# A latent-attention block with 16 tiles: two spreads as VectorE block transposes instead of TensorE products, and the scaling by one over the sums on VectorE behind the addition

## The reference, cut to what matters

```python
x = x + xattn(layernorm(x), ctx)       # 16 heads of 32; keys = values = context rows; softmax over 257
x = x + self_attn(layernorm(x), ...)   # low-rank q and kv, rope, 16 heads of 32, softmax over 32
x = x + ffn(layernorm(x), ...)         # 8 experts, each row takes the one with the largest gate

# xattn, per batch and head:
sim  = q @ k.T * 32 ** -0.5            # 32 x 257
out  = softmax(sim) @ k                # 32 x 32
```

## Time and profile before

| | |
|---|---|
| time, median of 3 runs | 858.45 us (856.07 to 860.0) |
| the profiled execution: span from its first to its last instruction | 854.9 us |
| what lies around that span, against the median | 3.5 us |
| mean granted clock of TensorE over the span | 0.984 of full speed |
| the chain that ended last, by engine | PE 61%, DVE 16%, POOL 7%, issue 6%, ACT 4%, DMA 3% |
| transfers from and to HBM | 151 GB/s over the span |

### The profile page before, as it was taken

The page is one execution under the profiler, slowest core; times in us unless marked ns, Lnnn a source line. Parts: engine busy times, 40 slices in busy tenths (PEclk is TensorE's granted clock), DMA queues, the critical chain, the costliest instruction groups (busy, mean ns, idle before and its releaser), DMA issues.

```text
span 854.9 us, 26663 instructions
## 1 busy us (share of the span) xinstructions
PE 768.7 (90%) x10666; PEld 577.6 (68%) x10666; DVE 610.8 (71%) x1211; ACT 422.9 (49%) x1062; POOL 313.9 (37%) x638
## 2 busy tenths in 40 slices
PE   4897979989899898988989899898988789999998
PEld 3544767768676786867768676786876556666664
DVE  3477677777877768787777877778645557788883
ACT  2353464554645556464554645546322354555552
POOL 2013533333234242333233234243220435876642
PEclk9999999999999999999999999999999899999999
DMA  9955654656646565484554636564061499454430
GB/s 277 331 130 100 132 153 118 143 140 130 153 112 160 124 162 138 100 184 120 148 142 117 163 110 152 128 159 101 3 222 51 140 375 388 163 172 140 144 115 3
DMA packets 113850, 129.16 MB, mean 151 GB/s; under 512 B 13951, under 2 KB 80767, under 8 KB 113729
## 3 DMA queue, kind: packets, MB, share of 16 engines
q1 hardware_dynamic: 105984, 109.35, 47.7%
q0 software_dynamic: 5520, 16.26, 5.6%
q10 hardware_dynamic: 2224, 1.86, 0.8%
HBM read 114.85 MB, written 14.42 MB: 151 GB/s over the span
## 4 chain that ended last, share of the span: by engine, by line
PE 61%; DVE 16%; POOL 7%; issue 6%; ACT 4%; DMA 3%; SPq 3%; DVEq 0%; POOLq 0%
PE bank L500 10%; PE bank L1560 8%; PE bank L502 8%; PE bank L501 8%; PE bank L494 4%; PE scores L541 3%; PE scores L551 3%; PE bank L565 2%; PE scores L1538 2%; PE scores L1540 2%; PE scores L1539 2%; DVE negmax L1031 2%; PE bank L605 2%; POOL soft L1315 2%; POOL operand_lo L1292 2%
## 5 line engine op out<-in xcount | busy, mean ns | idle before, releaser
L826 ACT ACTIVATE prob<-scores,negmax 128x257 f32<-128x257 f32 x256 | 118.2, 477 | 42.0 <-DVE negmax L1031 41.3
L500 PE MATMUL bank<-qkv_hi,operand_hi 128*128 128x396 f32 x256 | 99.3, 388 | 4.3 <-DVE operand_lo L1035 4.2
L1031 DVE TENSOR_REDUCE negmax<-scores 128x2 f32<-128x514 f32 x128 | 82.1, 683 | 22.2 <-PE scores L541 22.2
L1021 DVE STREAM_TRANSPOSE k_t<-keys 128x512 f32<-128x512 f32 x128 | 88.3, 691 | 5.6 <-DMA keys<-in_ctx 5.5
L501 PE MATMUL bank<-qkv_lo,operand_hi 128*128 128x396 f32 x256 | 88.1, 344 | 0.0
L502 PE MATMUL bank<-qkv_hi,operand_lo 128*128 128x396 f32 x256 | 87.8, 343 | 0.0
L1560 PE MATMUL bank<-w_all,hidden 128*128 x184 | 82.8, 592 | 0.6 <-ACT hidden L1613 0.6
L551 PE MATMUL scores<-consts,prob 128*128 128x128 f32 x512 | 77.6, 276 | 1.6 <-ACT prob L826 1.6
L565 PEld LDWEIGHTS bank<-prob_t,context 128*32 128x32 f32 x4096 | 47.0, 113 | 42.9 <-issue 34.9
L1656 DVE TENSOR_TENSOR w_lo<-w_all,w_hi 128x512 fp32r<-128x512 f32 x89 | 73.3, 882 | 0.2
L551 PEld LDWEIGHTS scores<-consts,prob 128*128 128x128 f32 x512 | 63.2, 144 | 9.6 <-ACT prob L826 2.5
(11 more groups left out here) (249 smaller groups left out, 1705.5 us busy)
## 6 DMA issues: line engine op xcount, KB each, us to landing
keys<-in_ctx SPq DMA_DIRECT2D x256, 128.0 KB, 4.4
context<-in_ctx SPq DMA_DIRECT2D x64, 512.0 KB, 4.6
w_all<-in_L_ffn_W SPq DMA_DIRECT2D x16, 1024.0 KB, 12.3
b<-in_L_ffn_b SPq DMA_DIRECT2D x23, 256.0 KB, 3.6
norm_scratch<-norm SPq DMA_DIRECT2D x16, 256.0 KB, 2.0
x_tile<-in_x SPq DMA_DIRECT2D x8, 256.0 KB, 4.9
x_pair<-in_x SPq DMA_DIRECT2D x8, 256.0 KB, 4.7
x_scratch<-x_tile SPq DMA_DIRECT2D x8, 256.0 KB, 2.5
```

Source lines behind the costliest of these rows:

```text
L500: pe.matmul(to, op_hi[op][:, c, :], w_hi[name][:, c, columns], start=(c == 0), stop=False)
L826: act.activation(prob[pair][:, gg, :], scores[:, g, 0:J], ACT.Exp, bias=negmax[b % 2][:, g:g + 1], accum_out=sums[t % 2][:, g, bl:bl + 1]) ...
L1021: dve.transpose(dst, src).then_inc(keys_turned, 1)
L1031: dve.tensor_reduce(negmax[b % 2][:, 2 * pair:2 * pair + 2], scores[:, 2 * pair:2 * pair + 2, 0:J], AX.X, ALU.max, negate=True).then_inc(m ...
```

## The change

The spreads leave TensorE. VectorE's block transpose, which turns each block of 32 x 32, reads a source in which one column is repeated 32 times, so that its result has each number in all 32 rows of a block: the inverses at offset -3 (`SPREAD_INV`, into `inv_t`) and the last key's probabilities at offset 0 (`SPREAD_LAST`, into `last_w`). GpSimd multiplies the latter by the last key at offset 1 (`WEIGH_LAST`), and VectorE adds the attention's bank and multiplies by the inverse in one go at offset 2 (`ATT`). `PLACE_LAST`, `PLACE_INV`, `ATT_INV`, the table `samehead` and two more small tables go. Because a block transpose keeps the block of 32 partitions, the attention's result and XOUT's weights use another order of heads (`place` instead of `hl`), and the last key's rows are turned a second time in that order (`turn_last(1)`, 16 small products, at step 0) and copied by ScalarE at step 1. XOUT moves from offset 10 to 8; `ATT_LO` has offset 4 instead of 2, which changes nothing in GpSimd's order.

```diff
-(INVERT, PLACE_LAST, PLACE_INV, X_BIAS, SPREAD, SPREAD_INV, ATT, ATT_INV, ATT_HI, ATT_LO, XOUT, X1, ...
+(INVERT, SPREAD_INV, SPREAD_LAST, WEIGH_LAST, X_BIAS, ATT, ATT_HI, ATT_LO, XOUT, X1, ...
-    -5, 0, -5, -6, 3, 3, 3, 4, 4, 2, 10, 17, ...
+    -5, -3, 0, 1, -6, 2, 4, 4, 8, 17, ...
...
-        "latent": (p[:, None] % S == np.arange(S)[None, :]),
-        "ofbatch": (p[:, None] // S == np.arange(BT)[None, :]),
-        "samehead": (p[:, None] // HD == p[None, :] // HD),
...
@@ attend, TensorE @@
-                        done = pe.matmul(att_bank[hl * HD:(hl + 1) * HD, at:at + S], context[b % 4][:, c, h * HD:(h + 1) * HD],
+                        done = pe.matmul(att_bank[place * HD:(place + 1) * HD, at:at + S], context[b % 4][:, c, h * HD:(h + 1) * HD],
...
@@ stages, TensorE @@
-            t = tile_at(step, SPREAD)
-            if t >= 0:
-                bank = bank_for("spread", t)
-                until.wait_ge(tables_made, 3)
-                until.wait_ge(plast_placed, t + 1)
-                for g in range(G):
-                    done = pe.matmul(bank[:, g * P:(g + 1) * P], samehead[:, g, :, :].rearrange("p h d -> p (h d)"),
-                                     op_plast[:, g, :, :].rearrange("p b i -> p (b i)"), start=True, stop=True)
-                done.then_inc(spread_done, 1)
-            t = tile_at(step, SPREAD_INV)
-            if t >= 0:
-                bank = bank_for("inv", t)
-                until.wait_ge(inv_placed, t + 1)
-                for g in range(G):
-                    done = pe.matmul(bank[:, g * P:(g + 1) * P], samehead[:, g, :, :].rearrange("p h d -> p (h d)"),
-                                     op_inv[:, g, :, :].rearrange("p b i -> p (b i)"), start=True, stop=True)
-                done.then_inc(inv_spread, 1)
...
+        def turn_last(placed):
+            for g in range(G):
+                for to in range(HL):
+                    h, at = ((to ^ g) if placed else to) * G + g, (placed * G + g) * B
+                    done = pe.matmul(last_bank[to * HD:(to + 1) * HD, at:at + B], last_rows[0:B, h * HD:(h + 1) * HD], ident[0:B, 0:B],
+                                     start=True, stop=True)
+            done.then_inc(last_turned, 1)
...
@@ ScalarE @@
+            if step == LAST_PLACED_AT:
+                until.wait_ge(last_turned, 2)
+                act.activation(last_p[:, :, :].rearrange("p g b -> p (g b)"), last_bank[:, G * B:2 * G * B], ACT.Copy).then_inc(last_ready, 1)
...
@@ stages, VectorE @@
+            t = tile_at(step, SPREAD_INV)
+            if t >= 0:
+                until.wait_ge(inverted, t + 1)
+                until.wait_ge(att_used, t)
+                until.wait_ge(unit_done, UNITS.index(("bias", 1)) + 1)
+                dve.transpose(over_head(inv_t), per_head(inv)).then_inc(inv_spread, 1)
+            t = tile_at(step, SPREAD_LAST)
+            if t >= 0:
+                until.wait_ge(plast_kept, 2 * BT * (t + 1))
+                until.wait_ge(att_added, t)
+                until.wait_ge(unit_done, len(UNITS))
+                dve.transpose(over_head(last_w), per_head(plast[t % 2])).then_inc(last_spread, 1)
             t = tile_at(step, ATT)
             if t >= 0:
-                until.wait_ge(spread_done, t + 1)
-                until.wait_ge(last_ready, 1)
+                until.wait_ge(last_weighed, t + 1)
                 until.wait_ge(att_hi, t)
                 until.wait_ge(att_lo, t)
-                last = last_t[:, :, BT * t:BT * t + BT].unsqueeze(3).broadcast_to([P, G, BT, S])
-                dve.tensor_tensor(grid4(att_w), grid4(banks[bank_of["spread"]]), last, ALU.mult).then_inc(spread_used, 1)
                 until.wait_ge(attended, 2 * (BT * t + BT))
-                until.wait_ge(spread_used, t + 1)
-                dve.tensor_tensor(att_w[:, :], att_w[:, :], att_bank[:, :], ALU.add).then_inc(att_added, 1)
-            t = tile_at(step, ATT_INV)
-            if t >= 0:
+                dve.tensor_tensor(att_w[:, :], last_w, att_bank[:, :], ALU.add).then_inc(att_added, 1)
                 until.wait_ge(inv_spread, t + 1)
                 until.wait_ge(att_added, t + 1)
-                dve.tensor_tensor(att_w[:, :], att_w[:, :], banks[bank_of["inv"]][:, :], ALU.mult).then_inc(att_used, 1)
+                dve.tensor_tensor(att_w[:, :], att_w[:, :], inv_t, ALU.mult).then_inc(att_used, 1)
...
+        def per_head(t_):
+            return t_[:, :, :].rearrange("p g b -> p (g b)").unsqueeze(2).broadcast_to([P, G * BT, HD])
+        def over_head(t_):
+            return t_.rearrange("p (n i) -> p n i", i=S)
...
@@ step TABLES_AT, VectorE @@
-                for g in range(G):
-                    for hl in range(HL):
-                        from_ = 2 * P + (hl ^ g) * HD
-                        done = dve.tensor_copy(samehead[:, g, hl, :], tables[:, from_:from_ + HD])
-                done.then_inc(tables_made, 1)
...
@@ stages, GpSimd @@
-                pool.tensor_tensor(op_plast[:, :, :, :], plast[t % 2][:, :, :].unsqueeze(3).broadcast_to([P, G, BT, S]), lat,
-                                   ALU.mult).then_inc(plast_placed, 1)
...
-                pool.tensor_tensor(op_inv[:, :, :, :], inv[:, :, :].unsqueeze(3).broadcast_to([P, G, BT, S]), lat, ALU.mult).then_inc(inv_placed, 1)
+            t = tile_at(step, WEIGH_LAST)
+            if t >= 0:
+                until.wait_ge(last_ready, 2)
+                until.wait_ge(last_spread, t + 1)
+                weight = last_p[:, :, BT * t:BT * t + BT].unsqueeze(3).broadcast_to([P, G, BT, S])
+                pool.tensor_tensor(grid4(last_w), grid4(last_w), weight, ALU.mult).then_inc(last_weighed, 1)
```

More of the change, by code:

```diff
@@ L87 @@
 TABLES_AT = 17
+LAST_PLACED_AT = 1
 BIAS_LOAD_AT = 8
@@ L231, in program @@
     v_w = [v0, v1]
-    op_plast = late[:, 5, :].rearrange("p (g b i) -> p g b i", g=G, b=BT)
+    last_w = late[:, 5, :]
     k_block = sba("k_block", [P, G, BT, HL, S])
@@ L366, in emptied_unit @@
         return {"down": down_moved, "k": k_summed, "bias": bias_moved}[kind], c + 1
-    bank_of = {"queries": 0, "spread": 0, "xout": 0, "norm": 1, "qkv0": 1, "qkv2": 1, "out": 2, "inv": 1, "gate": 0, "av": 0, "qkv1": 2, "q": 1, "k": 0, "norm3": 1, "rank": 0, "qkv3": 0, "self": 1}
-    step_of = {"queries": QUERIES, "spread": SPREAD, "inv": SPREAD_INV, "xout": XOUT, "norm": TURN1, "qkv0": QKV, "qkv1": QKV + 4, "qkv2": QKV + 8, "qkv3": QKV + 12,
+    bank_of = {"queries": 0, "xout": 0, "norm": 1, "qkv0": 1, "qkv2": 1, "out": 2, "gate": 0, "av": 0, "qkv1": 2, "q": 1, "k": 0, "norm3": 1, "rank": 0, "qkv3": 0, "self": 1}
+    step_of = {"queries": QUERIES, "xout": XOUT, "norm": TURN1, "qkv0": QKV, "qkv1": QKV + 4, "qkv2": QKV + 8, "qkv3": QKV + 12,
                "q": TURN_Q, "k": TURN_K, "self": SELF, "av": AV, "out": OUT, "norm3": TURN3, "gate": GATE, "rank": RANK}
@@ L376, in stage_step @@
         return step_of[stage] + TILE * (t + 1) + (later_of.get(stage, (0, 0))[t - T + 2] if t >= T - 2 else 0)
-    emptied = {"queries": queries_placed, "spread": spread_used, "inv": att_used, "xout": x1_made, "norm": norm_lo, "q": q2_moved, "self": soft_shifted, "av": self_lo,
+    emptied = {"queries": queries_placed, "xout": x1_made, "norm": norm_lo, "q": q2_moved, "self": soft_shifted, "av": self_lo,
                "out": x2_made, "norm3": x3_moved, "gate": gate_used, "rank": rank_used}
@@ L446, in sync_program @@
         load_context(3)
-        a, b = const_at["latent"][0], const_at["rope"][1]
+        a, b = const_at["rope"]
         sp.dma_start(consts_1[:, :], ins["const"][:, a:b]).then_inc(tables_loaded, 16)
-        a, b = const_at["before"][0], const_at["samehead"][1]
+        a, b = const_at["before"][0], const_at["all"][1]
         sp.dma_start(tables[:, 0:b - a], ins["const"][:, a:b]).then_inc(tables_loaded, 16)
@@ L581, in set_up @@
                 for o in range(G):
-                    for hl in range(HL):
-                        h = hl * G + c
-                        done = pe.matmul(bank[hl * HD:(hl + 1) * HD, o * P:(o + 1) * P], staged_a[:, o, h * HD:(h + 1) * HD], ident, start=True, stop=True)
+                    for place in range(HL):
+                        h = (place ^ c) * G + c
+                        done = pe.matmul(bank[place * HD:(place + 1) * HD, o * P:(o + 1) * P], staged_a[:, o, h * HD:(h + 1) * HD], ident, start=True, stop=True)
             if kind == "down":
@@ L606, in set_up @@
             if kind == "bias":
-                until.wait_ge(tables_made, 3)
+                until.wait_ge(tables_made, 2)
                 for k in range(2):
@@ L749, in stages @@
                 pe.matmul(bank[:, E:2 * E], before_and_all[:, 1, :], chosen_one[:, :], start=True, stop=True).then_inc(rank_done, 1)
+        def turn_last(placed):
[5 more added lines that the diff above has]
+            done.then_inc(last_turned, 1)
         turn_queries(0)
         until.wait_ge(last_loaded, 16)
-        for g in range(G):
-            for hl in range(HL):
-                h = hl * G + g
```

(7 more changed lines are left out.)

37 lines of the change are left out of this document (11 added, 26 removed).

## The result

The changed kernel takes **896.93 us** (median; 893.49 to 899.74) against 858.59 us for the kernel before in the same session (856.07 to 860.0): ratio 1.0449, 95% interval 1.0415 to 1.0483. The profiled execution took 894.92 us, its span is 893.0. Forecast: 891.5 us, range 868 to 902.

What follows compares the result with a forecast made beforehand. VectorE's and ScalarE's chains to XOUT were taken to bound the tile boundary; 14 x (1.2 + 1.2) = 33.6, last +1.0, start -1.4 give +33.2 on the 854.9 us span: 888.1, plus 3.5 around it, 891.5 us, range 868 to 902.

Steps and rivals of the forecast that it cites:

- What bounds the boundary: Between tiles VectorE and ScalarE set the pace, not TensorE, so the removed products gain nothing at 15 boundaries.
- The chain: Transposes ahead of X2's statistics delay X2, norm scaling, exponentials, ATT_HI and XOUT by 1.0 us per boundary.
- XOUT's steps, maxima, X1: Three XOUT parts now precede the next scores; X1 follows the maxima, so X1 and QKV start 1.2 us later.
- The clock: TensorE idles before XOUT and drops to 1.2 GHz: 1.5 us where it falls, four boundaries of five, 1.2 us.
- The start: The 16 samehead copies between a DMA's landing and the cut go, which gives 1.4 us.
- The first boundary: No k_block, X2 or softmax ahead and its clock already fallen: 0, between -1.5 and +0.5.
- The last boundary: It has no next scores behind it: +1.0 us.
- The QKV stretch unchanged: From the QKV products to the next boundary TensorE is the bound, and the stretch keeps its length.
- (a): Rival: the chain moves as forecast but the clock holds at the boundaries, +16.4, 875 us; chance 0.23.
- (b): Rival: faster, transposes covered by VectorE's idle time and XOUT earlier, 0.7 to 2.9 us per tile, 840 us; chance 0.12.
- (c): Rival: same time, XOUT's new place and freed TensorE give the delay back before QKV, 858 +- 4; chance 0.07.
- (d): Rival: two-SBUF operands or a repeated source cost VectorE 0.4 to 1.3 us more per tile, 897 to 912; chance 0.06.

Runs made afterwards that it cites:

- x_fewer: The kernel before, with one product instead of four in each of the two spreads per tile, no transpose added and no order changed: 869.34 us.
- x_early: The changed kernel with both transposes moved to step 40, where VectorE waits (first tile's second one left in place): 878.07 us.
- x_warm: The changed kernel with 12 unread TensorE products added per tile, eight at step 3 and four ahead of XOUT's first part: 874.42 us.
- x_early_warm: The changed kernel with the transposes at step 40 and nine unread products (six and three) in TensorE's gaps: 860.77 us.
- x_xout10: The changed kernel with XOUT back at offset 10, so one of its parts stands before the next batch's scores: 875.39 us.

## Why the prediction was right in sign and nearly in size

By its own steps:

- **What bounds the boundary**: right. Removing products was costed at nothing. x_fewer shows that it is even worth less than nothing.
- **The chain** (1.0 us per boundary): mis-sized, it is 0.79 in the changed kernel. The mechanism held link by link: k_block +0.37 (0.3 to 0.4 forecast), the norm's scaling +1.07 (1.0), and x_early gave back 1.05 by the place alone. The step that was wrong is "too late to help ScalarE" for the attention step that leaves VectorE, and with it that the two chains arrive together: ScalarE could start the high part 0.53 us behind the exponential but started 0.70 behind it in the kernel before, so the high part moved by 0.89 only, and XOUT by 0.79. With the transposes out of the way XOUT starts 0.26 earlier than before (x_early, 10.71 against 10.97).
- **XOUT's steps, maxima, X1** (1.2 in all, so 0.2 beside the chain; its own steps, 336.0 + 1.85 against 336.72, give 1.13): right in mechanism, too small. X to Q with the clock held is 11.40 against 11.03, 0.37. Chain and order together are 1.16 for a forecast of 1.2; the two errors cancel, which is luck. The scores came 2.7 us behind XOUT by forecast, and 4.8 in the trace, at half the clock.
- **The clock** (1.5 where it falls, at four boundaries of five, 1.2): right in mechanism, too small. It fell at all 13 and near the first and last as well. X to Q is 12.86 against 11.40 with the clock held, 1.46 us. So the price where it falls was right and how often it falls was not. The price was met by other parts than forecast: not 3.3 us of low clock wholly on the chain, but 6.8, of which 3.3 lay between X and Q in the mean at less than half a us each, and the rest ahead of XOUT at next to nothing. In the same way "the forecast 880 (the clock falls at every other boundary)" is a slip: 14 x (1.2 + 0.75) - 0.4 is 26.9, so 885.
- **The start** (-1.4): half. At the first cut of XOUT's weights it was -0.87 only: the copies' 1.4 us went, but what released VectorE landed 0.5 us later. At the scores ahead of XOUT of tile 1, the first row before, the second after, -0.69 is left. That XOUT of tile 1 is at -1.45, the number forecast, is luck: the other 0.76 arises between those scores and XOUT, where the two spreads no longer stand ahead of the attention's result, and at Q of tile 1 all of it is lost again (88.94 against 88.84).

```profile
66.85 0.80 PE L541 MATMUL scores<-k_t,q_t 32*32 32x257 f32 x32
66.16 0.80 PE L538 MATMUL scores<-k_t,q_t 32*32 32x257 f32 x32
```

- **The first boundary** (0): right as a number, and its reason failed. The clock did fall further there: 6.8 us from 72.4, 2.7 us ahead of XOUT, for 3.4 us from 77.3 before, and X to Q went from 12.31 to 13.86. But a second low stretch follows in both, 87.6 to 91.0 before and 86.1 to 89.5 here. Before it lay on the first QKV products, here mostly ahead of them, so Q to K is 0.73 shorter, and K of tile 2 comes 0.63 us earlier than before. From -0.69 to -0.63, the first boundary cost under 0.1 us.
- **The last boundary** (+1.0): measured +2.76 by XOUT of tile 16, of which 1.5 lie between X and Q of tile 15, in the forecast's own 14; the chain's part is 11.16 - 9.88 = 1.28.
- **The QKV stretch unchanged**: right within 0.1 us (2.72 - 0.79 - 1.83).

Sum: forecast +33.2 on the span, measured +38.1. Taken at the scores of the start and at K, where the forecast's terms part: start -0.7 (-1.4 forecast), first boundary +0.1 (0), 14 boundaries from K of tile 2 to K of tile 16 +37.5, 2.68 each (33.6, 2.4 each), the last +1.3 (1.0). So of the 4.9 us that are missing 3.9 lie in the 14 boundaries, 0.28 each, and the largest part of that, 0.26, is the clock at every boundary instead of four in five (1.46 for 1.2). The step of the sum that failed is how often the clock falls.

The rivals. (a) was about the right price for the case that it names: x_warm, which holds the clock, takes 874.4 us for the 875 worked out. The near match has some luck in it: a period is 1.33 us longer than before for the 1.2 worked out, and XOUT of tile 2 comes 2.5 us earlier for 1.4, with the clock held between XOUT and Q of tile 1 too, all but the last 1.0 us. (b) needed the transposes in a wait of VectorE; with that and the clock held the time is that of before (x_early_warm), not 840, since the removed products were never on the path. What it gains at XOUT is 0.26 us per tile, where 0.7 to 2.9 were named. (c) fell, as X1 follows the scores. (d) fell by its rows. Here are the groups of the two transposes and of the two attention steps in the changed kernel, over the whole span:

```profile
L1055 DVE STREAM_TRANSPOSE late<-plast 128x512 f32<-128x512 f32 x16 | 11.4, 711 | 0.5
L1049 DVE STREAM_TRANSPOSE staged_c<-inv 128x512 f32<-128x512 f32 x16 | 11.2, 702 | 0.0
L1065 DVE TENSOR_TENSOR late<-late,staged_c 128x512 f32<-128x512 f32 x16 | 11.1, 692 | 1.7
L1062 DVE TENSOR_TENSOR late<-late,bank 128x512 f32<-128x512 f32 x16 | 10.9, 679 | 0.0
```

A transpose with a repeated source costs 702 and 711 ns, 10 to 20 more than the keys'; the product from two SBUF operands costs 692, 13 more than the sum with one in PSUM. GpSimd was idle as it ran, from the root's end at 342.5 to 346.44, so these rows say nothing for or against the shut-out that the Trainium skill states (SBUF — State Buffer, "two separate sides").

## What to carry to other kernels

Products on TensorE that stand in a time in which it would wait are not load but cover: before they are taken away, read what is left between its waits, and price the low clock on what comes next and is on the path. An operation moved to another engine costs its *place* there: the same two transposes cost 1.05 us per tile ahead of a statistic that GpSimd and then ScalarE wait for, and nothing in a wait one and four steps earlier. And an earlier start is worth only what the next thing behind it in the order of the engine gains: look at the scores behind XOUT, not at XOUT.

## What the runs showed of the hardware that was not expected

Near the boundaries the low stretches were 3.4 or 6.8 us long in all these kernels, but for one of 10.2 us in x_xout10, and one arrangement could give either from tile to tile: in x_early they alternate, and most periods are 36.7 or 38.3 to 38.9. Where it falls decides its price: at one boundary of the changed kernel 4.5 us of low clock lay between XOUT and QKV (X to Q 13.4), at the next 2.4 (12.5), with none it is 11.4 (x_warm). So, as an estimate from these rows, a us of low clock in that stretch costs about 0.45 us in the changed kernel, and ahead of it, on groups of transposes that wait for ScalarE and GpSimd anyway, nearly nothing. The rate is not general: in x_xout10, whose scores stand behind one part of XOUT, 1.8 to 2.1 us of it right behind X cost 0.2 to 0.3 (11.25 to 11.38 against 11.07). What makes one arrangement recover earlier than another stays open.
